# A vision tower with soft mixture-of-experts: logits made by slot from tokens scaled to unit length, dispatch and slot inputs one step later

## The chip, the cores and the metric

One core of a Trainium2 chip. The metric is the device time of one launch in microseconds (us), the median of several runs on the same chip. TensorE is called PE in the rows, VectorE DVE, ScalarE ACT, GpSimd POOL; SP issues transfers.

## What is computed

64 images of 3x224x224 are cut into 196 patches of 16x16 and embedded to 192 features; then come one attention with decay, one layernorm, and a soft mixture of 64 experts ("slots"), with one more layernorm. The change lies in the mixture:

```python
xn = _rms_norm(x, norm_weight, RMS_EPS)
tok = _l2_normalize(xn)
sl = _l2_normalize(slots) * scale[:, None]
logits = jnp.einsum('sd,btd->bst', sl, tok)
dispatch_w = jax.nn.softmax(logits, axis=-1)      # over the tokens
combine_w = jax.nn.softmax(logits, axis=-2)       # over the slots
y = jnp.einsum('btd,bst->bsd', xn, dispatch_w)
y = jnp.einsum('sio,bsi->bso', fc1_weight, y) + fc1_bias
y = jax.nn.gelu(y, approximate=False)
y = jnp.einsum('sio,bsi->bso', fc2_weight, y) + fc2_bias
out = jnp.einsum('bsd,bst->btd', y, combine_w)
```

In front of it: `h = layernorm(h + attention(h))`; behind it: `layernorm(h + out)`. All inputs and outputs are fp32.

## The kernel before

Three phases follow each other. **Phase 1** is a loop of 32 steps, each on one pair of images (392 tokens, in four tiles `t` of 98). It is written as a software pipeline: step `i` embeds pair `i` and runs its attention, projects out and normalizes pair `i-1`, and makes the logits and both softmaxes of pair `i-2`; some of the leftovers are of pair `i-3`. Steps 0 to 3 and 31 are written out, 4 to 30 are a hardware loop; a step's flags `c`, `d`, `e` say whether pairs `i-1`, `i-2`, `i-3` exist. **Drain** (`drain` on PE, the code behind `phase1` on the others) finishes the last two pairs, 30 (`one`) and 31 (`last`). **Phase 2** runs the 64 experts in 32 steps of two, each with 2.3 MB of weights from HBM through a ring of six buffers. **Phase 3** mixes the expert outputs back to the tokens and normalizes.

There is no scheduler: the order on each engine is the order of the code, an engine takes its instructions in that order, and engines meet by semaphores (`pe.wait_ge(hb_sb, i + 1)` holds PE and all that stands behind it). Matmul results lie in the eight banks of `ps`; a bank can be written again only when its reader is done, so many waits are for a copy on ACT or DVE.

The steps of the mixture for one pair, with the lines of before:

- `tokens` (DVE): `gn` = (t2 - mean) times the norm weight; `squares` (ACT, L679) sums its squares; `token_norms` and `cosine_scales` on DVE with powers on POOL (`token_scales`, `inverse_norms` L496) make `amp` (rms scale) and `cosc` (scale to unit length).
- `token_features` (PE, L1279): eight transposes of `gn` into banks 6 and 7; ACT copies them to `tokT`.
- `logits` (PE, L1288): per tile two products with 98 tokens stationary and 64 slots moving, so the result lies by token; `cosines` (DVE) multiplies by `cosc` into `Lt`; `logits_turned` (L1295) turns it by slot.
- `slot_maxima`, `slot_exponentials`: `Es` = exp(logits - max) by slot; `dispatch_turned` (L1301) turns `Es` to tokens, ACT copies it to `DT`; `slot_inputs` (L1309) is the product of `DT` with `xn` (the tokens times `amp`, made by `scaled_tokens` on POOL); ACT scales it to `ysb`; `slot_inputs_turned` (L1263, L1265) turns it for phase 2, and ACT copies it to `yT`.
- `shifted_logits`, `token_exponentials`, `token_sums`, `combine_weights`: the softmax over slots, `Cn`; `combine_turned` (L1272) turns it, ACT copies it to `cst` (L716), SP stores it.

Of the attention around them: `hb` (DVE, L1003) frees banks 6 and 7; `scores` (PE, L1210) three times a step, each followed by a `decay` (DVE, L927) of 98x1568 elements, each followed by `values` (PE, L1243); `gate` (PE, L1156) with its Tanh on ACT (`gt`, L656); `keys_turned` (L1217); `carried` (L1257). ACT also rounds x for the next pair in two halves (`round_x`, L595) and loads a function table twice a step (`use_table`, L607). `idle_products` are matmuls without a use, put into gaps of the drain.

Of the kernel before, what the change touches and what calls it, by code (L numbers as in the profile page):

```python
# [24 lines left out]
TOK = GRID * GRID  # L25
# [44 lines left out]
def vit_tower(nc, xT, W, Wq, Wk, Wv, Wo, Wg1, Wg2, log_slope, row_slope, ln_w, ln_b, slots, scale, fc1, fc1b, fc2, fc2b,  # L70
# [6 lines left out]
    with ExitStack() as ctx:  # L77
# [109 lines left out]
        ss, nra, nrb, nrm, invn, cosc = (sb(n, [T, 4]) for n in ("ss", "nra", "nrb", "nrm", "invn", "cosc"))  # L187
        expo = sb("expo", [128, 4, 4])
# [4 lines left out]
        Lt, Lc, Ec, Cn = (sb(n, [T, 4, S]) for n in ("Lt", "Lc", "Ec", "Cn"))  # L193
# [38 lines left out]
        nra_rdy, nrm_rdy, invn_rdy, cosc_rdy = (sem(n) for n in ("nra_rdy", "nrm_rdy", "invn_rdy", "cosc_rdy"))  # L232
        h2_stored = sem("h2_stored")
        tokT_mm, tokT_sb = sem("tokT_mm"), sem("tokT_sb")
        lg_mm, Lt_rdy, lneg_rdy = sem("lg_mm"), sem("Lt_rdy"), sem("lneg_rdy")
# [39 lines left out]
        def phase3(eng, step):  # L275

            for n in range(DEEP):
                step(n, n, 0)
            with eng.Fori(1, NP // DEEP) as w:
                for n in range(DEEP):  # L280
                    step(DEEP * w + n, n, w)

# [129 lines left out]
        def _(pool):  # L412
# [43 lines left out]
            def step(i, c, d, e, f, more):  # L456
# [5 lines left out]
                if d:  # L462
                    scaled_tokens(i - 2)
# [3 lines left out]
                if d:  # L467
                    inverse_norms(i - 2)
# [47 lines left out]
            def scaled_tokens(j):  # L516

                pool.wait_ge(ra_rdy, j + 1)
                pool.wait_ge(gn_rdy, 4 * j + 4)
# [63 lines left out]
        def _(act):  # L583
# [25 lines left out]
            def step(i, c, d, e, f, more):  # L609
# [9 lines left out]
                if d:  # L619
                    act.wait_ge(tokT_mm, i - 1)  # L620
                    act.activation(tokT[:, :, :], ps[0:G, 6:8, 0:PT], ACT.Copy).then_inc(tokT_sb, 1)
# [4 lines left out]
                act.activation(hTh[:, 1], hT[:, 1], ACT.Copy).then_inc(hTh_rdy, 1)  # L626
                if more:
# [916 lines left out]
```

## Time and profile before

| | |
|---|---|
| time, median of 3 runs | 1163.93 us (1162.79 to 1168.42) |
| the profiled execution | 1163.77 us, its span 1162.0 us |
| loop, 100 to 800 us: busy | PE 691.93, DVE 586.77, ACT 531.02, POOL 467.58 of 700; granted clock 1.00 |
| drain, 850 to 879 us: busy | PE 23.84, DVE 17.30, ACT 14.66, POOL 12.84 of 29; granted clock 0.98 |
| of it, 862 to 864 us | PE 0.70 of 2; granted clock 1.00 |
| experts, 879 to 1058 us: busy | PE 176.79 of 179; DMA share 0.95, 383 GB/s |
| last stage, 1058 to 1162 us: busy | DVE 80.39, ACT 59.54, POOL 56.92, PE 51.25 of 104 |

A row of a timeline gives start and duration in us, the engine, the line, the operation, what it writes and reads, and in brackets how long the engine had stood idle before it and for whom. An fp32 product with a 64x192 result counts as two matmuls there. Matmuls overlap, so the time that a group takes on PE is better read from its start to the start of the next group than from its duration.

### The profile page before, as it was taken

What the parts mean: (1) busy time and instruction counts of PE and PEld (TensorE: products, weight loads), DVE (VectorE), ACT (ScalarE), POOL (GpSimd) and SP (SyncE); (2) the same over time, 40 slices, a digit from 0 to 9 for tenths busy, and PEclk for the clock granted to TensorE, in tenths of its full rate; (3) what the DMA queues carried; (4) which work ended last, traced back from release to release, by engine and by line L of the source; (5) the groups of instructions that cost most, each with busy time, mean ns of one, the idle gap of its engine ahead of it and who ended that gap; (6) DMA issues with size and microseconds to landing.
All of it is one profiled execution on the core that took longest, in us unless ns stands there. A gap on an engine that the chain in (4) does not pass through costs nothing.

```text
span 1162.0 us, 35600 instructions
## 1 busy us (share of the span) xinstructions
PE 1080.2 (93%) x13250; PEld 853.4 (73%) x13250; DVE 839.9 (72%) x2118; ACT 725.5 (62%) x1712; POOL 633.6 (55%) x971
## 2 busy tenths in 40 slices
PE   7899999999999999999999999999998999996652
PEld 6688888888888888888888888888874555654331
DVE  5878888888888888888888888888872222223996
ACT  6457777777777777777777777777752111111666
POOL 4556666667666666667666666667641000001664
PEclk9999999999999999999999999999998999998555
DMA  4511221111111221111111221111085999995885
GB/s 160 206 54 54 87 70 66 55 55 55 55 55 55 81 75 66 55 55 55 55 55 55 79 77 66 55 55 55 15 344 183 421 424 424 423 415 151 254 256 178
DMA packets 50996, 158.50 MB, mean 136 GB/s; under 512 B 5659, under 2 KB 31665, under 8 KB 38645
## 3 DMA queue, kind: packets, MB, share of 16 engines
q1 hardware_dynamic: 33352, 145.11, 34.1%
q10 hardware_dynamic: 17600, 12.78, 3.5%
q8 instruction: 31, 0.51, 0.2%
q14 instruction: 13, 0.10, 0.0%
HBM read 132.25 MB, written 25.62 MB: 136 GB/s over the span
## 4 chain that ended last, share of the span: by engine, by line
PE 83%; DVE 8%; issue 3%; ACT 2%; POOL 1%; DVEq 1%; DMA 1%; ACTq 0%; SPq 0%; POOLq 0%
PE ps L1118 9%; PE ps L1119 8%; PE ps L1120 8%; PE ps L1210 7%; PE ps L1243 7%; PE ps L1439 6%; PE ps L1288 4%; PE ps L1458 4%; PE ps L1140 3%; PE ps L1194 3%; PE ps L1195 3%; DVE res L1088 2%; PE ps L1177 2%; PE ps L1463 2%; PE ps L1472 2%
## 5 line engine op out<-in xcount | busy, mean ns | idle before, releaser
L927 DVE TENSOR_TENSOR p_sb<-ps,dec 98x1568 f32<-98x1568 f32 x96 | 172.0, 1791 | 25.9 <-PE ps L1210 23.2
L436 POOL TENSOR_TENSOR xl<-x_sb,xh 128x392 fp32r<-128x392 f32 x186 | 188.2, 1040 | 0.0
L492 POOL TENSOR_TENSOR hTl<-hT,hTh 128x392 fp32r<-128x392 f32 x64 | 66.3, 1036 | 135.5 <-ACT hTh L693 103.0
L755 ACT ACTIVATE hg<-ps 128x768 f32<-128x768 f32 x32 | 25.9, 810 | 148.4 <-PE ps L1463 148.4
L875 DVE SCALAR_TENSOR_TENSOR t<-t,rstd,hb 98x192 f32<-98x192 f32 x128 | 85.9, 710 | 24.4 <-POOL rstd L503 24.4
L1080 DVE COPY y2st<-ps 128x192 f32<-128x192 f32 x32 | 11.4, 358 | 120.4 <-PE ps L1439 120.4
L552 POOL CAST pickb<-pick 128x128 fp32r (+1 forms) x32 | 9.4, 293 | 150.3 <-PE ps L1463 150.3
L530 POOL TENSOR_TENSOR Cn<-Ec,crec 98x256 f32<-98x256 f32 x32 | 20.7, 648 | 125.3 <-DVE crec L964 125.3
L1243 PE MATMUL ps<-p_sb,vpad 98*32 98x98 f32 x3072 | 85.6, 252 | 2.0 <-DVE p_sb L927 2.0
L772 ACT ACTIVATE o_sb<-res,nb,rstd 98x192 f32<-98x192 f32 x128 | 59.5, 535 | 44.4 <-DVE nb L1103 43.7
L1487 PE MATMUL ps<-y2b,cbuf 64*98 64x192 f32 x256 | 49.2, 536 | 37.6 <-POOL y2b L565 37.6
L1243 PEld LDWEIGHTS ps<-p_sb,vpad 98*32 98x32 f32 x3072 | 64.6, 110 | 26.4 <-issue 13.8
L607 ACT ACT_TABLE_LOAD x60 | 77.0, 1283 | 1.1
L595 ACT ACTIVATE xh<-x_sb 128x1176 fp32r<-128x1176 f32 x64 | 74.9, 1172 | 1.2 <-DMA x_sb<-in_xT 1.1
L686 ACT ACTIVATE h<-t,mur,ra 98x192 f32<-98x192 f32 x128 | 59.7, 538 | 23.5 <-DVE mur L907 21.8
L1487 PEld LDWEIGHTS ps<-y2b,cbuf 64*98 64x98 f32 x256 | 32.5, 266 | 54.1 <-issue 31.0
L1118 PE MATMUL ps<-xl,wh 128*128 128x392 f32 x192 | 69.6, 362 | 2.0 <-POOL xl L440 2.0
L1439 PEld LDWEIGHTS ps<-w2v,hgT 128*64 128x64 f32 x768 | 52.3, 137 | 25.9 <-issue 18.5
L1439 PE MATMUL ps<-w2v,hgT 128*64 128x192 f32 x768 | 69.5, 330 | 1.1 <-DVE hgT L1074 1.1
L1210 PE MATMUL ps<-qA,kA 32*98 32x196 f32 x1024 | 59.6, 345 | 10.1 <-ACT vpad L674 7.5
L1194 PE MATMUL ps<-xl,whl 128*128 128x392 f32 x192 | 68.1, 355 | 0.0
L523 POOL TENSOR_TENSOR xn<-gn,ra 98x192 f32<-98x192 f32 x128 | 68.1, 560 | 0.0
(221 smaller groups left out, 3443.6 us busy)
## 6 DMA issues: line engine op xcount, KB each, us to landing
x_sb<-in_xT SPq DMA_DIRECT2D x32, 1176.0 KB, 5.3
w1v<-in_fc SPq DMA_DIRECT2D x32, 1152.0 KB, 10.7
w2v<-in_fc SPq DMA_DIRECT2D x32, 1152.0 KB, 13.2
h_dram<-h SPq DMA_DIRECT2D x32, 294.0 KB
h2r<-h_dram SPq DMA_DIRECT2D x32, 294.0 KB
out<-o_sb ACTq DMA_DIRECT2D x32, 294.0 KB
comb_dram<-cst SPq DMA_DIRECT2D x32, 98.0 KB, 5.2
cbuf<-comb_dram SPq DMA_DIRECT2D x32, 98.0 KB, 4.0
```

The source lines that it names most:

```text
L436: pool.tensor_tensor(xl[:, k], x_sb[:, k], xh[:, k].bitcast(F32), ALU.subtract)\
L607: act.activation(warm[:, 1:2], warm[:, 0:1], func)
L875: dve.scalar_tensor_tensor(t2[0:T, t], t2[0:T, t], rstd1[:, t:t + 1], hb[0:T, t], ALU.mult, ALU.add).then_inc(t2_rdy, 1)
L927: dve.tensor_tensor(dst, src, rate.unsqueeze(2).to_broadcast([T, 4, 2, TOK]), ALU.mult)\
L1118: pe.matmul(out, hi, x_lo, start=start, stop=False)
L1119: pe.matmul(out, lo, x_hi, start=False, stop=False)
L1120: return pe.matmul(out, hi, x_hi, start=False, stop=stop)
L1194: pe.matmul(ps[:, 1, 0:PT], whl[:, k], xl[:, k], start=(k == 0), stop=False)
L1210: mm = pe.matmul(ps[0:T, SC_AT + r, mt * TOK:(mt + 1) * TOK].rearrange("p (b n) -> p b n", b=2), keys[rows, n], queries[rows, :, n], start ...
L1243: mm = pe.matmul(ps[32 * r:32 * r + 32, 6 + k // 2, at:at + T], vpad[:, 2 * a + mt, 32 * h:32 * h + 32], p_sb[:, k % 2, mt, (2 * r + odd) ...
L1439: mm = pe.matmul(ps[64 * s:64 * s + 64, 4 + n % 2, 0:D], hgT[:, k, at:at + 64], w2v[n][:, s, k], start=(k == 0), stop=(k == FJ - 1))
L1487: mm = pe.matmul(ps[0:T, 2 * n + a, k * D:(k + 1) * D], cbuf[64 * a:64 * a + 64, n, k * T:(k + 1) * T], y2b[64 * a:64 * a + 64, n, :], sta ...
```

## The change

- `cosines` and `Lt` are gone. POOL scales `gn` by `cosc` instead of `amp` (`unit_tokens` for `scaled_tokens`), so `xn` holds tokens of unit length; PE turns these, and the logits come out final. They are made by slot: 64 slots stationary, 196 tokens moving, two products for each of the two images (`logits(j, a)`), into bank 0.
- ACT copies the logits from bank 0 to `Es` (`logits_kept`); `slot_maxima` and the exponential work on `Es`; `logits_turned` now turns them to tokens into bank 1, for `shifted_logits`.
- The dispatch weights need the token's length back: DVE makes `size` in `cosine_scales`, and `dispatch_scaled` multiplies it into `DT` (it was a copy on ACT).
- In the loop `dispatch_turned` and `slot_inputs` of pair `i-3` move behind the two `project_out` calls of step `i`; `token_features` moves behind `hb`; `slot_inputs_turned` follows `combine_turned` between the turned keys and `scores` 1, and `gate` waits for ACT's copies of both; the turned keys go to bank 0; the second half of `round_x` moves behind Tanh on ACT.
- The drain is written anew: pair 29 ends there, pair 31 is scaled by DVE into `hb`, and the last `combine_turned` moves into the first expert step.

The core of the diff:

```diff
@@ POOL: step, unit_tokens @@
-                    scaled_tokens(i - 2)
+                    inverse_norms(i - 2)
                 low_h(i, 1)
                 if c:
                     first_norm(i - 1, 1)
                 if d:
-                    inverse_norms(i - 2)
+                    unit_tokens(i - 2)
...
-                    pool.tensor_tensor(xn[0:T, t], gn[0:T, t], amp[:, t:t + 1].to_broadcast([T, D]), ALU.mult)\
+                    pool.tensor_tensor(xn[0:T, t], gn[0:T, t], cosc[:, t:t + 1].to_broadcast([T, D]), ALU.mult)\
...
@@ POOL: drain @@
-            scaled_tokens(one)
+            unit_tokens(one)
             token_scales(last)
+            inverse_norms(last)
             combine_weights(one)
-            inverse_norms(last)
-            scaled_tokens(last)
             combine_weights(last)
@@ ACT: step @@
                 act.activation(hTh[:, 1], hT[:, 1], ACT.Copy).then_inc(hTh_rdy, 1)
+                if e:
+                    slot_inputs_scaled(i - 3)
...
+                if d:
+                    token_rows(i - 2)
                 if e:
-                    combine_kept(i - 3, 0, f)
-                if more:
-                    round_x(i + 1, 1)
+                    slot_inputs_kept(i - 3, 1, 0)
+                    combine_kept(i - 3, 1, f)
...
+                if more:
+                    round_x(i + 1, 1)
                 if d:
                     use_table(ACT.Exp)
+                    logits_kept(i - 2)
                     slot_exponentials(i - 2)
-                    if e:
-                        slot_inputs_kept(i - 3, 1, 0)
-                    dispatch(i - 2)
                     token_exponentials(i - 2)
...
+            def logits_kept(j):
+                act.wait_ge(lg_mm, j + 1)
+                if not (isinstance(j, int) and j == 0):
+                    act.wait_ge(dt_mm, j)
+                act.activation(Es[:, :], ps[:, 0, 0:TOK], ACT.Copy).then_inc(lg_sb, 1)
...
@@ ACT: drain, from the exponentials of pair 30 on @@
             token_exponentials(one)
             squares(last)
+            slot_inputs_scaled(one)
+            slot_inputs_kept(one, 5, 0)
             token_rows(last)
+            combine_kept(one, 4, True)
+            logits_kept(last)
+            slot_exponentials(last)
+            token_exponentials(last)
+            slot_inputs_scaled(last)
+            slot_inputs_kept(last, 5, 0)
             second_norm(last)
...
+            combine_kept(last, 6, True)
@@ DVE @@
+            def dispatch_scaled(j, norms):
+                dve.wait_ge(dt_mm, j + 1)
+                dve.wait_ge(size_rdy, j + 1)
...
+                dve.tensor_tensor(DT[:, :, :].rearrange("p k (a s) -> p k a s", a=2),
+                                  ps[0:T, 6, 0:256].rearrange("p (k a s) -> p k a s", k=2, a=2),
+                                  norms[:, :].rearrange("p (a k) -> p k a", a=2).unsqueeze(3)
+                                  .to_broadcast([T, 2, 2, S]), ALU.mult).then_inc(DT_sb, 1)
...
             for t in range(4):
+                dve.tensor_scalar(hb[0:T, t], gn[0:T, t], cosc[:, t:t + 1], None, ALU.mult).then_inc(xn_rdy, 1)
@@ PE: logits @@
-                        mm = pe.matmul(ps[0:T, 6 + t // 2, at:at + S], tokT[0:G, k, t * T:(t + 1) * T], slT[:, k, :],
-                                       start=(k == 0), stop=(k == 1))
+                for k in range(2):
+                    mm = pe.matmul(ps[64 * a:64 * a + 64, 0, 0:TOK], slT[:, k, :], tokT[0:G, k, a * TOK:(a + 1) * TOK],
+                                   start=(k == 0), stop=(k == 1))
@@ PE: step, from keys_turned on @@
                 if e:
-                    combine_turned(i - 3, 0)
+                    pe.wait_ge(zl_rdy, i + 1)
+                    pe.wait_ge(q_sb, 2 * i + 2)
+                    combine_turned(i - 3, 1)
+                    slot_inputs_turned(i - 3, 1, 0)
                 scores(i, 1, c)
+                pe.wait_ge(kts_rdy, i + 1)
                 if e:
+                    pe.wait_ge(yT_sb, 2 * i - 4)
                     pe.wait_ge(cb_sb, i - 2)
                 gate(i)
...
-                    logits_turned(i - 2)
+                    logits(i - 2, 0)
                 scores(i, 2, c)
+                if d:
+                    logits(i - 2, 1)
                 carried_ready(i)
                 values(i, 1)
...
                 carried(i, 0)
                 if d:
...
+                    logits_turned(i - 2)
                 values(i, 2)
...
                 carried(i, 1)
```

Where it moves instructions, as they stand in the loop. First PE behind `project_out` 0 (the products of woh and wol with og) and ahead of `embed` 1 (xl, xh with whl); before:

```order
L1177 MATMUL ps<-woh,ogl 98x192 x2
L1177 MATMUL ps<-woh,ogh 98x192 x2
L1276 ISA
L1279 MATMUL ps<-ident,gn 96x98 x8
L1194 MATMUL ps<-xl,whl 128x392
L1195 MATMUL ps<-xh,whl 128x392
```

After:

```order
L1194 MATMUL ps<-woh,ogl 98x192 x2
L1194 MATMUL ps<-woh,ogh 98x192 x2
L1317 MATMUL ps<-ident,Es 98x128 x2
L1211 MATMUL ps<-xl,whl 128x392
L1212 MATMUL ps<-xh,whl 128x392
```

Eight transposes of tokens are replaced by two of Es.

Second PE from `scores` 0 on (qA with kA); before:

```order
L1210 MATMUL ps<-qA,kA 98x196 x8
L1288 MATMUL ps<-slT,tokT 98x64 x8
L1217 MATMUL ps<-ident,kA 98x128 x2
L1218 MATMUL ps<-ident,kB 98x128
L1272 MATMUL ps<-ident,Cn 128x98 x2
L1204 ISA
L1210 MATMUL ps<-qA,kA 98x196 x8
L1156 MATMUL ps<-zs,gw 128x392
L1157 MATMUL ps<-zs,gw 64x392
L1243 MATMUL ps<-p_sb,vpad 32x98 x16
L1226 MATMUL ps<-vpad,kts 32x32 x12
L1295 MATMUL ps<-ident,Lt 128x98 x2
```

After:

```order
L1296 MATMUL ps<-ident,xn 96x98 x8
L1234 MATMUL ps<-ident,kA 98x128 x2
L1235 MATMUL ps<-ident,kB 98x128
L1289 MATMUL ps<-ident,Cn 128x98 x2
L1280 MATMUL ps<-ident,ysb 128x128
L1282 MATMUL ps<-ident,ysb 64x64 x2
L1221 ISA
L1227 MATMUL ps<-qA,kA 98x196 x8
L1381 REGISTER_ALU
L1173 MATMUL ps<-zs,gw 128x392
L1174 MATMUL ps<-zs,gw 64x392
L1260 MATMUL ps<-p_sb,vpad 32x98 x16
```

Between `scores` 0 and 1 the turned tokens and the turned ysb stand where the eight products of the logits stood; the new logits follow further on, ahead of and behind `scores` 2.

Third ACT from the second half of q (qB) to the Exp table; before:

```order
L645 ACTIVATE qB<-ps,parity 64x196 x4
L714 ISA
L716 ACTIVATE cst<-ps 128x196
L595 ACTIVATE xh<-x_sb 128x1176
L656 ACTIVATE gt<-ps 128x392
L659 ACTIVATE gt<-ps 64x196 x2
L607 ACT_TABLE_LOAD
```

After:

```order
L646 ACTIVATE qB<-ps,parity 64x196 x4
L674 ACTIVATE tokT<-ps 96x784
L731 ISA
L731 ACTIVATE yT<-ps 128x2x64
L731 REGISTER_ALU
L731 ACTIVATE yT<-ps 128x2x32
L724 REGISTER_ALU
L726 ACTIVATE cst<-ps 128x196
L658 ACTIVATE gt<-ps 128x392
L661 ACTIVATE gt<-ps 64x196 x2
L597 ACTIVATE xh<-x_sb 128x1176
L609 ACT_TABLE_LOAD
```

tokT and yT come ahead of cst, and the rounding of x goes behind Tanh.

## Rows read from the trace of the kernel before

**Rows 1.** Timeline of PE, one step; columns as told under the profile.

```profile
526.60 1.60 PE L1288 MATMUL ps<-slT,tokT 96*98 96x64 f32 x16
528.04 0.38 PE L1217 MATMUL ps<-ident,kA 128*98 128x128 f32 x2
...
529.48 0.44 PE L1156 MATMUL ps<-zs,gw 80*128 80x392 f32 x1
...
531.04 0.39 PE L1295 MATMUL ps<-ident,Lt 98*128 98x98 f32 x2
531.46 0.92 PE L1210 MATMUL ps<-qB,kB 32*98 32x196 f32 x16
...
533.13 0.33 PE L1263 MATMUL ps<-ident,ysb 128*128 128x128 f32 x1
...
533.66 0.54 PE L1257 MATMUL ps<-qd,state 32*32 32x98 f32 x16
534.13 0.43 PE L1301 MATMUL ps<-ident,Es 128*98 128x128 f32 x2
534.49 0.88 PE L1243 MATMUL ps<-p_sb,vpad 98*32 98x98 f32 x32
535.30 0.87 PE L1309 MATMUL ps<-xn,DT 98*64 98x192 f32 x8
536.10 0.37 PE L1257 MATMUL ps<-qd,state 32*32 32x98 f32 x8
...
540.79 0.88 PE L1279 MATMUL ps<-ident,gn 98*96 98x98 f32 x8
541.45 0.42 PE L1194 MATMUL ps<-xl,whl 128*128 128x392 f32 x1
```

**Rows 2.** Timelines of DVE and PE in step 0, and one decay of the steady step.

```profile
27.59 1.79 DVE L927 TENSOR_TENSOR p_sb<-ps,dec 98x1568 f32<-98x1568 f32 x1 [0.19 <-PE ps L1210]
...
35.27 0.89 PE L1243 MATMUL ps<-p_sb,vpad 98*32 98x98 f32 x32 [0.79 <-DVE p_sb L927]
...
526.63 1.79 DVE L927 TENSOR_TENSOR p_sb<-ps,dec 98x1568 f32<-98x1568 f32 x1
```

**Rows 3.** Timeline of ACT in the same step as rows 1.

```profile
526.08 1.47 ACT L645 ACTIVATE qB<-ps,parity 64x196 f32<-64x196 f32 x4
528.80 0.33 ACT L716 ACTIVATE cst<-ps 128x196 f32<-128x196 f32 x1 [1.25 <-PE ps L1272]
529.03 1.18 ACT L595 ACTIVATE xh<-x_sb 128x1176 fp32r<-128x1176 f32 x1
530.10 0.49 ACT L656 ACTIVATE gt<-ps 128x392 f32<-128x392 f32 x1
...
531.15 1.28 ACT L607 ACT_TABLE_LOAD   x1
...
533.85 0.51 ACT L721 ACTIVATE yT<-ps 128x128 f32 x2 [0.81 <-PE ps L1265]
...
542.61 0.81 ACT L621 ACTIVATE tokT<-ps 96x784 f32<-96x784 f32 x1
```

**Rows 4.** Timeline of DVE in step 0, a tensor-scalar operation.

```profile
35.04 0.35 DVE L825 TENSOR_SCALAR woh<-wo 128x384 fp32r<-128x384 f32 x1
```

**Rows 5.** Timelines of PE and DVE in the drain and the first expert step.

```profile
863.30 0.43 PE L1301 MATMUL ps<-ident,Es 128*98 128x128 f32 x2 [1.38 <-ACT Es L697]
...
868.55 0.16 DVE L899 TENSOR_TENSOR nra<-ss,ra 98x4 f32<-98x4 f32 x1 [3.70 <-ACT ysq L679]
...
871.41 0.46 DVE L911 TENSOR_TENSOR cosc<-ra,invn 98x4 f32<-98x4 f32 x1 [1.69 <-POOL invn L496]
...
878.19 0.56 PE L1272 MATMUL ps<-ident,Cn 98*128 98x98 f32 x2 [1.10 <-POOL Cn L530]
...
880.17 2.83 PE L1458 MATMUL ps<-w1v,yT 128*64 128x384 f32 x8
```

**Rows 6.** Windows: stretch, its length, busy PE, PEld, DVE, ACT, POOL, granted clock, DMA.

```profile
878.00:879.00 1.00, 0.56 (x2) 0.29 (x2) 0.00 (x0) 0.16 (x1) 0.88 (x5) 0.53 0.00 0
```

More of the change, by code:

```diff
@@ L1045, in _ @@
                 dve.tensor_tensor(ogl[:, n], og[:, n], ogh[:, n].bitcast(F32), ALU.subtract).then_inc(ogl_rdy, 1)
+            dispatch_scaled(one - 1, size)
             tokens(one)
@@ L1050, in _ @@
             residual(last, 0)
-            cosine_scales(one)
-            cosines(one)
+            cosine_scales(one, size)
             residual(last, 1)
@@ L1055, in _ @@
             residual_statistics(last, 1)
+            tokens(last)
             slot_maxima(one)
-            tokens(last)
+            shifted_logits(one)
             slot_sums(one)
-            shifted_logits(one)
             token_norms(last)
+            dispatch_scaled(one, size)
             mean_shifts(last)
             token_sums(one)
-            cosine_scales(last)
-            cosines(last)
+            cosine_scales(last, size_last)
+            dve.wait_ge(cosc_rdy, NP)
+            for t in range(4):
+                dve.tensor_scalar(hb[0:T, t], gn[0:T, t], cosc[:, t:t + 1], None, ALU.mult).then_inc(xn_rdy, 1)
             slot_maxima(last)
@@ L1067, in _ @@
             slot_sums(last)
+            dispatch_scaled(last, size_last)
             token_sums(last)
@@ L1183, in embed @@
                     pe.wait_ge(g_sb, 2 * i - 1 + g)
-                if e and g == 1:
-                    pe.wait_ge(y_sb, i - 2)
+                if e:
+                    pe.wait_ge((lg_sb, Lc_rdy)[g], i - 2)
                 for k in range(KP):
@@ L1333, in step @@
                     project_out(i - 1, 0)
-                if d:
-                    token_features(i - 2)
+                if e:
+                    dispatch_turned(i - 3)
                 embed(i, 1, c, e)
@@ L1338, in step @@
                     project_out(i - 1, 1)
+                if e:
+                    slot_inputs(i - 3, xn)
                 if at_start(i):
@@ L1389, in drain @@
                 one, last = NP - 2, NP - 1
-                idle_products(0, 8)
+                pe.wait_ge(og_sb, 2 * NP)
+                dispatch_turned(one - 1)
+                idle_products(0, 7)
                 project_out(last, 0)
-                token_features(one)
+                slot_inputs(one - 1, xn)
                 project_out(last, 1)
-                combine_turned(one - 1, 0)
-                slot_inputs_turned(one - 1, 0, TOK)
-                logits(one)
-                idle_products(1, 6)
+                pe.wait_ge(Lc_rdy, one)
+                combine_turned(one - 1, 1)
+                slot_inputs_turned(one - 1, 1, 0)
+                idle_products(0, 6)
+                token_features(one, xn)
+                idle_products(0, 4)
+                logits(one, 0)
+                logits(one, 1)
+                pe.wait_ge(t1_rdy, 4 * NP)
+                idle_products(2, 2)
+                pe.wait_ge(yT_sb, 2 * one)
                 pe.wait_ge(cb_sb, one)
-                pe.wait_ge(yT_sb, 2 * one)
                 logits_turned(one)
-                idle_products(1, 8)
+                idle_products(2, 5)
                 dispatch_turned(one)
-                idle_products(1, 2)
-                slot_inputs(one)
-                pe.wait_ge(t1_rdy, 4 * NP)
+                idle_products(2, 2)
+                slot_inputs(one, xn)
+                idle_products(2, 2)
                 slot_inputs_turned(one, 5, 0)
-                idle_products(2, 8)
-                token_features(last)
+                idle_products(2, 3)
+                token_features(last, hb)
                 idle_products(2, 4)
-                logits(last)
+                logits(last, 0)
+                logits(last, 1)
                 combine_turned(one, 4)
-                idle_products(2, 2)
+                pe.wait_ge(Lc_rdy, one + 1)
                 logits_turned(last)
```

161 lines of the change are left out of this document (69 added, 92 removed).

## The prediction, made before the changed kernel ran

> **What bounds the kernel now.** I read the page first: its slices and the share of TensorE say that the first 850 us, a loop of 32 steps of some 26 us, keep TensorE busy without a break. Then I read one step in the timeline of TensorE [rows 1] and looked, for every break between its stretches, at what the other engines had just finished. The reader is to see two kinds of stretch in it. From `values` 2 at 534.49 through both `embed` calls to the projections, matmuls follow each other with no gap: whatever is taken out there shortens the step by as much. From the end of `hb` (where `logits` starts, 526.60) to `values` 2 (534.49) lie 7.89 us in which DVE runs three `decay` operations of 1.79 us, each waiting for `scores` and each waited for by the next `scores` or `values`. Step 0, where TensorE has little else to do, shows what that chain takes alone: from 27.59, where the first decay starts, to 35.27, where `values` 2 starts, 7.68 us [rows 2]; in the steady step the same stretch takes 7.86, from the decay at 526.63 [rows 2] on. So this window is 0.18 above its floor: filled with work on TensorE, and nearly as long without it. I call it the window; zero of its clock is 526.60.
>
> **What the change does to the path outside the window.** `token_features` leaves it: 540.79 to 541.45, 0.66. `dispatch_turned` comes in behind `project_out` 0: 534.13 to 534.49, 0.36. `slot_inputs` goes from behind `values` 2 to behind `project_out` 1: 535.30 to 536.10, 0.80, on the path in either place. Together -0.30 us a step. Nothing covers these products, so the gain is real if TensorE finds no new wait there. The new waits: `slot_inputs` needs DT, which is now a DVE multiplication of 256 columns behind `first_norm` 0 (the multiplication that made Lt, of the same size, goes); between `dispatch_turned` and `slot_inputs` TensorE runs `embed` 1 and `project_out` 1, over 3 us (from 541.45 on), and the multiplication has room. `h_turned` 1 needs `y_sb`, behind `hTh` on ACT, with the first half of the projections as cover. On POOL the scaling of four tiles moves behind `low_h` 1 and the inverse norms in front of it; POOL is busy two thirds of the time there, and the scaled tokens are wanted only after `hb`. I cost all these at nothing; without cover the DT wait would cost about what it now hides, up to 0.5 a step.
>
> **What it does inside the window.** Out go the old `logits` (526.60 to 528.04: 1.44) and the turning of Lt (531.04 to 531.46: 0.42). In come `token_features` (0.66) and the new `logits`: four products of a 64-column stationary tile with 196 moving columns instead of eight with 64. The nearest row is `slot_inputs`, four products of 64 stationary and 192 moving columns: 0.80. One pair of transposes of Es (0.36) leaves and another takes its place. TensorE's work in the window falls by 0.40, to 7.49. But 7.49 is under the 7.68 of the decays, so no more than 0.18 can be had here, and two new round trips to ACT decide how much:
>
> First, `gate` now waits until ACT has copied tokT, yT and cst. qB ends at 526.08 + 1.47 = 0.95 on the window's clock; tokT 0.81 more: 1.76 [rows 3]. TensorE ends `slot_inputs_turned` at 0.66 + about 0.55 (turned keys and combine weights: 528.04 to 529.48 less the 0.9 of `scores`) + 0.53 (533.13 to 533.66) = 1.75; yT began 0.19 after that point before, so 1.94, plus 0.51 and 0.33: 2.7 to 2.8, and with a hand-off 2.85. Before, `gate` started at 529.48 = 2.88. Even.
>
> Second, `logits_turned` needs the copy of the logits, behind two Tanh, the rounding of x and the table load on ACT. From `gate`: 0.62 to Tanh (530.10), 1.05 to the end of both (531.15), 1.07 for x (529.03 to 530.10), 1.28 and a little more for the table, 0.33 for a copy like cst: 7.3, with a hand-off 7.45. TensorE gets there at 2.85 + 1.56 (529.48 to 531.04) + 0.40 + 1.67 (531.46 to 533.13) + 0.40 + 0.47 (533.66 to 534.13) = 7.35. It waits 0.1, turns the logits in 0.36 and starts `values` 2 at 7.83 against 7.89.
>
> So the window gives -0.06, between -0.18 (the decays alone) and whatever ACT is late by. A step is 0.36 shorter. The 29 steps from 3 to 31 have it in full, step 2 has only the 0.66 of `token_features`: 29 x 0.36 + 0.66 = **11.1 us** off the loop; with -0.18 in the window 29 x 0.48 + 0.66 = 14.6.
>
> Here the Trainium skill speaks against a simple reading: "Trainium Kernel Development and Optimization", section Performance Expectations, calls the busy time of matmuls a bad metric, because they are pipelined. By busy time alone the 0.7 a step taken from TensorE would all be gain, 20 us; by the rule a busy TensorE proves no bound at all, and the change could be worth nothing (the second rival is that case). The decays of [rows 2] side with the rule inside the window and not outside it.
>
> **The last passage** (from the loop's end to the first weights). For the last pair the order is now serial: norms, scaling, turning, copy, logits, copy, where before turning and logits ran beside the norms. From cosc on there are four scalings on DVE, 0.66 of transposes, tokT 0.81, logits 0.80 and a copy 0.33. A scaling of 192 columns lies under the 0.35 of 384 columns [rows 4], over the 0.16 of a 4-column row [rows 5]; I take 0.27, 1.1 for four. With five hand-offs and the idle products in between that is 5.4, less 0.5 for the multiplication it replaces: +4.9. Against it, cosc comes sooner: DVE waited 3.70 for the squares and 1.69 for the inverse norms [rows 5], both of which now stand ahead of work for pair 30 on ACT and POOL; I estimate -2.8 of these 5.4. The turning of the last combine weights (a wait of 1.10, and about 0.5 more for cst) moves into the first weights' products: -1.6; added idle products ahead of the end: +1.7. The granted clock had fallen to 0.53 by 878 to 879 [rows 6], and the eight first weights' products at 880.17 took 2.83 [rows 5]. With idle products in the gaps I expect the full level and half the time for them and their like: -2.2. Then ACT, ahead of the first Gelu: four h2 rows, cst, the table load (1.28, [rows 3]): +1.3. Sum +1.3; nearer to +1 since the loop's last `slot_inputs` no longer stands ahead of the last og.
>
> One gap in it is new: pair 30's scaled tokens come from POOL only after its cosc, and I make TensorE idle there for nearly 3 us, against 1.38 at 863.30 [rows 5], after which the granted clock stayed at 1.00 (the table of the profile section), and 1.10 at 878.19, by when it had fallen. I take it that the clock falls there to the lower level, 1.2 instead of 2.4 GHz: turning and logits at twice their 0.66 and 0.80 and idle products in front of them, some +2. So the passage costs **+3 us**, with bounds of -2 (no fall, nearly all 5.4 of the waits gone) and +6.
>
> The Trainium skill, "VectorE: DVE Perf Modes", section Mode 2x_2P, lets an fp32 tensor-scalar run at two results a cycle; the 0.35 for 384 columns agrees. By it the four scalings would be some 0.3 us cheaper.
>
> After that nothing changes: the weights' products and the last stage start later or earlier as a block, since each transfer of weights follows a product. The comb store moves behind the first products; its reload was issued some 10 us ahead of use.
>
> **Sum.** Profiled execution 1163.77 (span 1162.0; the median of the three runs is 1163.93, the same): 1163.8 - 11.1 + 3 = **1155.7 us**.
>
> **Rivals.**
> 1. The window reaches its floor and the clock does not fall: 1163.8 - 14.6 + 0 = 1149. For it: the work is under the floor. Against: the margin at the two round trips is 0.1.
> 2. The window grows by what the outside gives. ACT now does three copies between qB and Tanh and the rounding of x between Tanh and the table; hand-offs of 0.1 more at each, or DVE late for `hb`, put `values` 2 at 8.1 to 8.2 instead of 7.83. Then a step gains 0 to 0.1 and the passage is left: 1163.8 - 2 + 1 = 1163, within 0.5%.
> 3. Slower: ACT takes over the window. Each 0.1 by which `gate` comes after 2.85 moves `scores` 2, the last decay and `values` 2 by 0.1. From a `gate` at 3.2 on the loop gains nothing; at 3.5, if tokT, yT and cst each need a further 0.2, a step is 0.3 longer: 1163.8 + 29 x 0.3 - 0.66 + 1 = 1173. The rows have tokT behind qB without a gap, so I hold it unlikely.
> 4. The logits are not cheaper: at their old 1.44 TensorE would need 8.13 in the window, +0.24 against 7.89, and the step would gain 0.06: 1165, even. The row of `slot_inputs` speaks against it.
>
> **How the numbers follow.** Forecast 0.50, first rival 0.16, second and fourth 0.24, third 0.10. The range takes in the bounds of window and passage and the second rival, and leaves out the third and the edge of the first: 1147 to 1165. A difference of 0.5%, 5.8 us, is about what a measurement here can tell from none. Faster than 1158: most of the forecast and the first rival, 0.65; within: 0.25; slower than 1169.7: 0.10.
>
> **What would show it.** In the step after: the time from one step's `logits` to the next's 0.36 less; `token_features` behind `hb` without a wait; `gate` 2.85 after it; ACT's copy of the logits just ahead of `logits_turned`; no wait ahead of `slot_inputs`. In the passage: a TensorE gap near 3 us ahead of pair 30's `token_features` with the granted clock falling behind it, and the first weights at full clock. Wrong: waits of TensorE for ACT of more than 0.2 in each step, or the first weights' products not some 7 us earlier than 880.17.

## The result, and the profile after

The changed kernel takes 1191.26 us (median, 1190.01 to 1192.63) where the kernel before took 1165.84 (1162.79 to 1168.42) beside it: a ratio of 1.0216, interval 1.0194 to 1.0238. It is slower by some 25 us; the forecast was 1155.7, in a range of 1147 to 1165. The profiled execution of after has a span of 1188.3 us.

One steady step on PE, timeline of after (as [rows 1]), from the end of `hb`:

```profile
514.97 0.88 PE L1296 MATMUL ps<-ident,xn 98*96 98x98 f32 x8 [0.90 <-DVE hb L1018]
...
517.63 0.41 PE L1173 MATMUL ps<-zs,gw 80*128 80x392 f32 x1
...
519.15 0.88 PE L1303 MATMUL ps<-tokT,slT 96*64 96x196 f32 x4
519.96 0.92 PE L1227 MATMUL ps<-qB,kB 32*98 32x196 f32 x16
520.81 0.88 PE L1303 MATMUL ps<-tokT,slT 96*64 96x196 f32 x4
521.62 0.89 PE L1260 MATMUL ps<-p_sb,vpad 98*32 98x98 f32 x32
...
522.91 0.42 PE L1311 MATMUL ps<-ident,Es 128*98 128x128 f32 x2
523.26 0.89 PE L1260 MATMUL ps<-p_sb,vpad 98*32 98x98 f32 x32
...
528.79 0.42 PE L1317 MATMUL ps<-ident,Es 128*98 128x128 f32 x2
528.97 0.42 PE L1211 MATMUL ps<-xl,whl 128*128 128x392 f32 x1
...
540.10 0.92 PE L1227 MATMUL ps<-qA,kA 32*98 32x196 f32 x16 [0.23 <-ACT vpad L686]
...
541.92 0.87 PE L1296 MATMUL ps<-ident,xn 98*96 98x98 f32 x8 [0.91 <-DVE hb L1018]
```

The rows of before that go with it, besides [rows 1], are `values` 2 of one step and `scores` 0 of the next:

```profile
508.32 0.88 PE L1243 MATMUL ps<-p_sb,vpad 98*32 98x98 f32 x32
...
525.66 0.92 PE L1210 MATMUL ps<-qA,kA 32*98 32x196 f32 x16 [0.23 <-ACT vpad L674]
```

A step takes 541.92 - 514.97 = 26.95 us; before it took 26.2 (from `values` 2 at 508.32 to 534.49). Three stretches make the difference of about +0.77:

- The window, from the end of `hb` (514.97) to `values` 2 (523.26): 8.29, against 7.89 in [rows 1]: **+0.40**. The two halves of `logits` take 0.81 each, 519.15 to 519.96 and 520.81 to 521.62, together 1.62.
- From `values` 2 to the next `scores` 0 (540.10): 16.84, against 17.34 before (508.32 to 525.66): **-0.50**.
- From `scores` 0 to the end of the wait for `hb` (541.92): 1.82, against 0.94 before: **+0.88**, a wait of 0.9 that was not there. The waits of PE from 300 to 800 us list it in 18 steps (us in total, times, longest):

```profile
PE ps L1296 <- DVE hb L1018: 16.3, 18, 0.9
```

Why DVE is late with `hb` stands in the same step's timelines of DVE and of POOL:

```profile
504.63 0.75 DVE L883 SCALAR_TENSOR_TENSOR t<-t,rstd,hb 98x192 f32<-98x192 f32 x2
...
507.33 0.81 DVE L920 TENSOR_TENSOR cosc<-ra,invn 98x4 f32<-98x4 f32 x1
...
510.23 2.17 DVE L883 SCALAR_TENSOR_TENSOR t<-t,rstd,hb 98x192 f32<-98x192 f32 x2 [0.38 <-POOL rstd L507]
512.33 0.61 DVE L889 BATCH_NORM_STATS2 st<-t 98x6 f32<-98x192 f32 x2
...
513.88 0.96 DVE L1018 TENSOR_TENSOR hb<-ps,lnb 98x768 f32<-98x768 f32 x1
```

```profile
504.61 1.01 POOL L500 TENSOR_TENSOR invn<-nrm,expo 98x4 f32<-98x4 f32 x1
507.08 1.04 POOL L496 TENSOR_TENSOR hTl<-hT,hTh 128x392 fp32r<-128x392 f32 x1 [1.46 <-ACT hTh L625]
509.15 0.19 POOL L505 TENSOR_TENSOR ve<-mv,expo 98x2 f32<-98x2 f32 x1 [1.03 <-DVE mv L871]
...
510.08 2.07 POOL L526 TENSOR_TENSOR xn<-gn,cosc 98x192 f32<-98x192 f32 x4
512.11 3.12 POOL L440 TENSOR_TENSOR xl<-x_sb,xh 128x392 fp32r<-128x392 f32 x3
```

`cosc` has four columns and took 0.153 in every steady step before; here it starts at 507.33, inside POOL's `hTl`, and ends with it, 0.81 later. What follows it on DVE comes later, POOL waits 1.03 for `mv`, and residual 1 waits for POOL's `rstd`. Then residual 1 itself, two tiles, takes 2.17 beside POOL's scaling; before, residual 1 took 1.51 and residual 0, which had the scaling beside it then, 1.15. The statistics at 512.33, with one operand in SBUF, take 0.61 beside POOL's `xl`, as they did without it.

Running side by side does not settle it alone. In the same step residual 0 takes only 0.75 for its two tiles (504.63) while POOL's inverse norms run (504.61, 1.01). And in every steady step of before `cosc` too starts inside an operation of POOL, the first of the three of `xl`, but 0.13 ahead of its end, and comes through. DVE in one step of before, then that one operation of POOL:

```profile
522.51 1.51 DVE L875 SCALAR_TENSOR_TENSOR t<-t,rstd,hb 98x192 f32<-98x192 f32 x2
...
524.80 0.15 DVE L911 TENSOR_TENSOR cosc<-ra,invn 98x4 f32<-98x4 f32 x1
```

```profile
523.77 1.16 POOL L436 TENSOR_TENSOR xl<-x_sb,xh 128x392 fp32r<-128x392 f32 x1
```

In the last passage the gap of nearly 3 us is there, and the first weights' products are at full clock (1.51, against 2.83 in [rows 5]). The granted clock stayed at 1.00 (4 us from 884) behind that gap and fell behind the next. Timeline of PE, then windows with the columns of [rows 6]:

```profile
885.08 0.88 PE L1296 MATMUL ps<-ident,xn 98*96 98x98 f32 x8 [2.98 <-POOL xn L526]
886.87 0.89 PE L1303 MATMUL ps<-tokT,slT 96*64 96x196 f32 x8
892.46 0.87 PE L1324 MATMUL ps<-xn,DT 98*64 98x192 f32 x8 [1.99 <-DVE DT L928]
...
907.00 1.51 PE L1482 MATMUL ps<-w1v,yT 128*64 128x384 f32 x8
```

```profile
884.00:888.00 4.00, 2.92 (x26) 2.43 (x27) 2.70 (x12) 1.00 (x2) 3.08 (x6) 1.00 1.00 424
892.00:896.00 4.00, 3.54 (x23) 2.82 (x24) 2.59 (x11) 0.92 (x3) 1.59 (x2) 0.71 0.40 150
```

From `values` 2 of the last step to the first turning of `hg` the passage takes 38.5 us (872.91 to 911.44), before 36.9 (848.49 to 885.41): +1.6. The loop has lost 24.4 (`values` 2 of the last step at 872.91 instead of 848.49); 24.4 + 1.6 = 26.0, and the spans differ by 26.3.

One more row matters here. In the passage both halves of `logits` stand together, and all four products take 0.82 from their start to the next group's (886.87 to 887.69): as much as one half alone in the loop.

### The profile page after: what moved, and what is told of

Read it like the earlier page. It is cut to its first block, busy times and chain, and to the rows that moved or that the text cites. A ratio compares the mean times of both kernels' runs of the same rounds, so it can differ in the third digit from the quotient of the medians.

```text
span 1188.3 us, 35236 instructions
## 1 busy us (share of the span) xinstructions
PE 1076.5 (91%) x13008; PEld 837.5 (70%) x13008; DVE 862.8 (73%) x2154; ACT 738.8 (62%) x1711; POOL 628.2 (53%) x967
## 4 chain that ended last, share of the span: by engine, by line
POOL 36%; issue 27%; PE 22%; DVE 10%; ACT 2%; DVEq 1%; DMA 1%; POOLq 1%; ACTq 0%; SPq 0%
POOL xl L440 14%; PE ps L1463 6%; POOL xn L526 5%; PE ps L1482 4%; POOL ra L517 4%; POOL hTl L496 4%; POOL rstd L507 2%; DVE res L1103 2%; POOL invn L500 2%; PE ps L1498 2%; DVE st L1109 2%; PE ps L1489 2%; POOL qd L477 1%; DVE p_sb L947 1%; PE ps L1227 1%
## 5 line engine op out<-in xcount | busy, mean ns | idle before, releaser
L883 DVE SCALAR_TENSOR_TENSOR t<-t,rstd,hb 98x192 f32<-98x192 f32 x128 | 93.1, 767 | 15.9 <-POOL rstd L507 15.5
L1463 PEld LDWEIGHTS ps<-w2v,hgT 128*64 128x64 f32 x768 | 52.3, 137 | 25.8 <-issue 18.5
L1133 PE MATMUL ps<-wvl,hTh 128*98 128x192 f32 x256 | 67.3, 263 | 0.2 <-DVE t L876 0.2
## 6 DMA issues: line engine op xcount, KB each, us to landing
w1v<-in_fc SPq DMA_DIRECT2D x32, 1152.0 KB, 11.1
```

The lines of the kernel that those rows point to most:

```text
L883: dve.scalar_tensor_tensor(t2[0:T, t], t2[0:T, t], rstd1[:, t:t + 1], hb[0:T, t], ALU.mult, ALU.add).then_inc(t2_rdy, 1)
L1133: pe.matmul(out, hi, x_lo, start=start, stop=False)
L1463: mm = pe.matmul(ps[64 * s:64 * s + 64, 4 + n % 2, 0:D], hgT[:, k, at:at + 64], w2v[n][:, s, k], start=(k == 0), stop=(k == FJ - 1))
```

## The experiments

My theory of the two losses: the halves of `logits` write different 64-column halves of the array and run side by side only when they are adjacent; and a DVE operation with two SBUF operands does not get through while POOL works on SBUF (the rows of residual 0 and of before's `cosc` show that this is too broad as it stands). The rivals: a product costs what it costs wherever it stands; and DVE is late because it has more operations in its queue.

**e1_join**: the two halves together.

```diff
+                scores(i, 2, c)
                 if d:
                     pe.wait_ge(g_sb, 2 * i + 1)
                     logits(i - 2, 0)
-                scores(i, 2, c)
-                if d:
                     logits(i - 2, 1)
```

> Both halves of the logits stand together behind the scores of the third heads, instead of one ahead of them and one behind. Theory A (two products that write different 64-column halves of the array run side by side when they are adjacent, and only then): the four products take 0.8 together as in the last passage, TensorE's work in the window falls by 0.8, the third scores start 0.45 earlier, and the window from the token features to values 2 falls from 8.29 to about 7.85; 29 steps x 0.45 = -13, about 1178 us. Theory B (a product costs 0.2 to 0.4 wherever it stands, and the window is long because of ACT's round trips): the four take 1.6 in their new place, and the time stays within 3 us of 1191.

Measured: 1179.39 us, ratio 1.0121 (1.0078 to 1.0164). Timeline of PE in the window:

```profile
432.47 0.92 PE L1227 MATMUL ps<-qB,kB 32*98 32x196 f32 x16 [0.26 <-DVE p_sb L947]
433.32 0.89 PE L1303 MATMUL ps<-tokT,slT 96*64 96x196 f32 x8
434.14 0.89 PE L1260 MATMUL ps<-p_sb,vpad 98*32 98x98 f32 x32
...
435.79 0.89 PE L1260 MATMUL ps<-p_sb,vpad 98*32 98x98 f32 x32
```

The four products take 0.82 together, though the code has both products of one half ahead of both of the other, and with `token_features` at 427.96 the window is 7.83 (to 435.79): theory A, 12 us of the 25.

**e2_cosc_early**: `cosine_scales` ahead of the statistics of residual 0, so ahead of POOL's `hTl`; on DVE nothing is added or removed.

```diff
+                if d:
+                    cosine_scales(i - 2, size)
                 if c:
                     residual_statistics(i - 1, 0)
-                if d:
-                    cosine_scales(i - 2, size)
```

> The inverse norms times amplitudes (cosc, size) are computed on DVE right behind the sum of h, ahead of the statistics of residual 0, so before POOL begins its low half of h; nothing is added or taken away on DVE. Theory A (cosc takes 0.80 because it runs against POOL's low half of h, and all of DVE up to hb is late by that): cosc takes 0.15, TensorE's wait of 0.90 for hb goes from 0.90 to 0.3 or less, a step gets 0.6 to 0.9 shorter, 29 x 0.6 to 0.9 = -17 to -26 us, 1165 to 1174. Theory B (DVE is late because two more small operations and the wait for POOL's inverse norms stand in its queue, wherever they stand): cosc still takes 0.8 or DVE waits for the inverse norms as long, and the time stays within 4 us of 1191.

Measured: 1173.6 us, ratio 1.0064 (1.0043 to 1.0086). `cosc` between 300 and 800 us (duration in ns: least, median, most), and PE's wait for `hb`:

```profile
L920 DVE TENSOR_TENSOR cosc<-ra,invn x19: 161/164/165, 311.1 to 784.1; 98x4 f32<-98x4 f32 x19
```

```profile
529.19 0.87 PE L1296 MATMUL ps<-ident,xn 98*96 98x98 f32 x8 [0.25 <-DVE hb L1018]
```

The same operation, 0.8 us earlier in the queue: 0.164 instead of 0.80, and a step 0.66 shorter (`scores` 0 from 501.74 to 528.02: 26.28). So it was its place beside POOL and not its being there.

**e3_join_cosc**: both edits.

> Both edits of the two runs before it. If the two losses are separate, one ahead of the window and one in it, the gains add: 29 x (0.45 + 0.6 to 0.87) = -30 to -38 us, 1153 to 1161, below the kernel before, near the forecast of 1155.7. If one of them only hides the other, the sum falls short of that by the smaller one: 1166 to 1178.

Measured: 1158.01 us (1157.31 to 1159.74), ratio 0.9932 (0.991 to 0.9954): faster than before, and 2.3 us from the forecast. PE:

```profile
495.55 0.87 PE L1296 MATMUL ps<-ident,xn 98*96 98x98 f32 x8 [0.25 <-DVE hb L1018]
...
503.38 0.89 PE L1260 MATMUL ps<-p_sb,vpad 98*32 98x98 f32 x32
...
521.37 0.88 PE L1296 MATMUL ps<-ident,xn 98*96 98x98 f32 x8 [0.24 <-DVE hb L1018]
```

The window is 7.83 and the step 25.82. From `values` 2 of step 0 to `values` 2 of step 31 the loop takes 804.2 us (34.78 to 839.00), after 836.7, e1 823.2, e2 816.8: -13.5 and -19.9 singly, -32.5 together. The two losses are separate.

**e4_same_half**: e1 with both halves on the same 64 columns of the array. The copy to `Es` still reads the old places, so half of the logits in its output are not those asked for.

```diff
-                    mm = pe.matmul(ps[64 * a:64 * a + 64, 0, 0:TOK], slT[:, k, :], tokT[0:G, k, a * TOK:(a + 1) * TOK],
+                    mm = pe.matmul(ps[0:64, 0, 256 * a:256 * a + TOK], slT[:, k, :], tokT[0:G, k, a * TOK:(a + 1) * TOK],
```

> As the run with both halves of the logits together, but both halves write the same 64 columns of the array (at other places of the bank); the copy reads the old places, so half of the logits in the output are not those asked for. Theory A (adjacent products on different column halves overlap): the four products take 1.6 from start to start again, though adjacent, and the time is about 1190. Theory C (what overlaps is only the latency of products that stand next to each other): they take 0.8 as with different halves, and the time is that of the run with both halves together.

Measured: 1200.18 us (one run). PE:

```profile
414.79 1.54 PE L1303 MATMUL ps<-tokT,slT 96*64 96x196 f32 x8
416.26 0.89 PE L1260 MATMUL ps<-p_sb,vpad 98*32 98x98 f32 x32
```

Adjacent, but on the same columns, they take 1.47. So it needs both: different column halves, next to each other. The time is 9 us above after, not at it as I expected. Some 6 of them lie in the loop (842.8 from `values` 2 of step 0 to that of step 31, in after 836.7): behind `scores` 2 the pair leaves PE waiting 0.27 for DVE's decay ahead of them, and in after the first half stood there. Another 4 lie in the last passage (42.65 against 38.5), which has the same edit and in which the granted clock fell twice.

**e10_join_ahead**: e3 with the pair ahead of `scores` 2.

> As e3_join_cosc, but both halves of the logits stand ahead of the scores of the third heads instead of behind them. Theory A (what the join saves is TensorE's work, 0.8 a step, wherever the pair stands): scores 2 start 0.55 later, but values 1 follow them at once, values 2 start within 0.1 of where they did, and the time is within 3 us of 1158. Theory B (what the join saves is that scores 2, and so the last decay on DVE, start earlier): the window grows by 0.4 to 0.55 a step again, 1170 to 1174.

Measured: 1161.18 us (1158.55 to 1164.63), ratio 0.9967 (0.9954 to 0.998). In its trace `scores` 2 start 0.48 later in the window than in e3, and `values` 2 at the same 7.83 (499.72 to 507.55). What the join saves is PE's work, not the place of `scores` 2; 1170 is ruled out. A step takes 0.06 more than e3's, and its wait for `hb` is 0.30 instead of 0.24. Of the 5.7 us between the two profiled executions 3.5 lie ahead of `values` 2 of step 0 (38.24, in e3 34.78), ahead of anything that the edit moves; whether the 3 us between the medians come from there is not shown.

**e7_pool_yields**: e3, and POOL waits in each step until residual 1 is done.

```diff
                 if c:
                     first_norm(i - 1, 1)
+                    pool.wait_ge(t2_rdy, 4 * i)
                 if d:
                     unit_tokens(i - 2)
```

> On top of e3_join_cosc: in each step POOL waits until DVE has done residual 1 before it scales the tokens; no work changes. Theory A (DVE's residual of two SBUF operands gets through only when POOL stands still, 1.1 for one beside the scaling against 0.41 alone): residual 1 takes 0.75 to 0.85 instead of 2.17, POOL starts the scaling 0.8 later, and TensorE's wait of 0.24 for hb goes to 0 to 0.1; 29 x 0.15 to 0.24 = -4 to -7 us, 1151 to 1154. Theory B (the residual is slow for another reason, such as its operands from ACT or PSUM traffic): it keeps its 2.17, hb waits as before, the scaling comes 2 later and the token features wait for POOL: above 1165.

Measured: 1152.47 us (1151.27 to 1157.12), ratio 0.9897 (0.9866 to 0.9927). The time is as expected and the place of the gain is not. Residual 1 takes 0.75 in every step and the wait for `hb` is gone from the list, but the steady step still takes 25.8: the first decay starts 0.98 after `scores` 0 in both kernels (516.75 after 515.77, 521.19 after 520.21), so it had waited for `scores`, and 0.24 of waiting for `hb` beside it cost nothing. From step 0 to 31 the gain is 5.5 us, and 4.5 of them lie in step 1, where POOL runs `xl` right behind `rstd`. DVE and POOL in step 1 of after, then DVE in step 1 of e7:

```profile
50.11 3.15 DVE L883 SCALAR_TENSOR_TENSOR t<-t,rstd,hb 98x192 f32<-98x192 f32 x1 [0.30 <-POOL rstd L507]
```

```profile
50.04 3.00 POOL L440 TENSOR_TENSOR xl<-x_sb,xh 128x392 fp32r<-128x392 f32 x3
```

```profile
49.50 0.75 DVE L884 SCALAR_TENSOR_TENSOR t<-t,rstd,hb 98x192 f32<-98x192 f32 x2 [0.31 <-POOL rstd L508]
```

One tile took 3.15 us beside three POOL operations in a row, and two take 0.75 without them.

**e9_before_yields**: the same wait in the kernel before, ahead of its first `split_x`.

> The kernel before with one wait more: in each step POOL waits until DVE has done residual 1 before it forms the first remainders of x. In the trace of e7_pool_yields the gain came in step 1 alone (residual 1 of step 1 took 3.83 beside those remainders and 0.75 with the wait), not in each step, and the trace of before has the same 3.83. Theory A (that loss belongs to both kernels, and the change under study has no part in it): the kernel before gains 3 to 4.5 us, to about 1162, so of e7's lead over before only what e3 has is the change's. Theory B (the wait only helps together with the scaling on POOL): within 1 us of before.

Measured: 1425.87 us (1369 to 1437, so that even the quickest of four is 204 above before): a large loss that neither theory named. Step 1 gains as expected (its residual 1 takes 0.75), and the other steps lose far more. DVE, POOL and PE in one step of the execution that took 1418.3 us:

```profile
632.76 3.30 DVE L913 TENSOR_TENSOR cosc<-ra,invn 98x4 f32<-98x4 f32 x1
```

```profile
632.50 2.98 POOL L436 TENSOR_TENSOR xl<-x_sb,xh 128x392 fp32r<-128x392 f32 x3
635.44 0.60 POOL L475 TENSOR_TENSOR qd<-qA 128x196 f32<-128x196 f32 x1
```

```profile
637.70 2.61 PE L1290 MATMUL ps<-slT,tokT 96*98 96x64 f32 x16 [2.27 <-DVE hb L1005]
```

The wait lets `xl` start behind residual 1 instead of beside it, so that `cosc`, two operations further on DVE, comes 0.26 behind the start of `xl`'s first operation and not, as in before, 0.13 ahead of its end. It takes 3.30, until the fourth POOL operation in a row ends; PE stands for 2.27; and behind such gaps the granted clock falls to the lower level. The gap of the step ahead took 2.35 and ended at 601.98; behind it the clock was low for some 17 us, 604 to 621. Windows from that gap on:

```profile
604.00:606.00 2.00, 2.00 (x18) 1.42 (x18) 1.12 (x3) 1.41 (x2) 0.43 (x2) 0.50 0.00 0
...
620.00:622.00 2.00, 2.00 (x10) 2.00 (x9) 1.38 (x5) 1.29 (x3) 0.00 (x0) 0.75 0.00 0
622.00:624.00 2.00, 2.00 (x22) 1.78 (x21) 0.40 (x2) 1.36 (x5) 0.26 (x1) 1.00 0.49 151
```

**e11_before_step1** and **e12_join_cosc_step1**: the wait in step 1 alone (`if c and not d:`), in the kernel before and in e3.

> The kernel before with POOL's wait for residual 1 in step 1 alone. Theory A (the 3.83 of residual 1 in step 1 is a loss of both kernels, and the 260 us of e9 came from the other steps, where the wait pushes POOL's remainders of x onto DVE's small cosc, 3.29 there): residual 1 of step 1 takes 0.75, step 1 ends 3 to 4 earlier, the rest is as before: 1161 to 1163. Theory B (the kernel before has cover for it): within 1 us of before.

> e3_join_cosc with POOL's wait for residual 1 in step 1 alone. Theory A (the wait of 0.24 for hb in the steady step hides nothing, since the first decay waits for the scores, and e7's gain was step 1's and step 2's): 3 to 4 us less than e3, 1153.5 to 1155, and the steady step as in e3. Theory B (e7 also gained in each step): no more than 1 us under e3's 1158.

Measured: e11 1161.9 us, ratio 0.9976 (0.9964 to 0.9989); e12 1154.41, ratio 0.9919 (0.9897 to 0.9941). Both as theory A had it: from `values` 2 of step 0 to that of step 31, e11 is 3.1 us under before (810.1 against 813.2), and e12 4.6 under e3 (799.6). The loss in step 1 belongs to both kernels; what the change and its two repairs bring by themselves is e3's 0.68%.

**e5_dve_scale** and **e6_squares_first**: the last passage, on top of e3. In e5 DVE scales pair 30 right behind `cosc`, with the `tensor_scalar` that pair 31 has. In e6 ACT makes the squares of pair 31 ahead of its copy of pair 30's logits.

```diff
@@ POOL @@
-            unit_tokens(one)
@@ DVE @@
             cosine_scales(one, size)
+            dve.wait_ge(cosc_rdy, NP - 1)
+            dve.wait_ge(y_mm, one)
+            for t in range(4):
+                dve.tensor_scalar(xn[0:T, t], gn[0:T, t], cosc[:, t:t + 1], None, ALU.mult).then_inc(xn_rdy, 1)
@@ ACT @@
             token_rows(one)
+            squares(last)
             logits_kept(one)
             slot_exponentials(one)
             token_exponentials(one)
-            squares(last)
```

> On top of the join and the early cosc (e3_join_cosc): in the last passage pair 30's four scalings go from POOL (2.19 in that run's trace, 851.12 at their end) to DVE right behind cosc (1.01 there for pair 31's), ahead of the last residual. Theory A (the passage is a chain, and TensorE's gap ahead of pair 30's token features is all POOL's scaling): the gap of 2.99 goes to 1.4 to 1.7, and if the granted clock then stays at 1.00, the 0.50 level of 852 to 856 goes too: from values 2 of the last step to the first turning of hg 39.74 becomes 36.3 to 38.3. Theory B (the chain of squares and norms of pair 31, pushed back 1 us on DVE, ends last): TensorE waits as much more at DT behind it, and the 39.74 stays within 0.5.

> On top of e3_join_cosc: in the last passage ACT makes the squares of pair 31 ahead of its copy of pair 30's logits instead of behind the exponentials. Theory A (TensorE's wait of 1.99 for DT is a wait for these squares, through the norms that stand ahead of DT on DVE): the wait goes to 0.3 to 0.6 and the passage of 39.74 to about 38.2. Theory B (the wait is the exponentials', turning and DVE multiplication's own latency): it stays above 1.5, and the copy of the logits behind the squares comes later.

Measured, one run each: 1155.78 and 1153.94 us. The passage, 39.7 in e3, takes 36.4 in e5 and 36.75 in e6. PE in e5, then in e6:

```profile
853.15 0.88 PE L1299 MATMUL ps<-ident,xn 98*96 98x98 f32 x8 [1.75 <-DVE xn L1066]
```

```profile
857.73 0.87 PE L1324 MATMUL ps<-xn,DT 98*64 98x192 f32 x8
```

The gap of 2.99 is 1.75 in e5, and the granted clock is 1.00 from 848 to 862. In e6 the wait for DT (1.99) is gone; the passage gains 3.0 where I had expected 1.5. Part of that goes with the clock, which came back sooner (0.50 for 852 to 854 only, in e3 from 852 to 856): e1 and e7, which have e3's passage, took 38.5 for it without either edit, and against these e5 gains 2.1 and e6 1.8. Of e5's shorter passage less is left in its time, since `values` 2 of step 0 comes at 38.32 there, 3.5 later than in e3, ahead of anything that the edit moves.

**e8_all**: e3 with the edits of e5, e6 and e7.

> The three edits before it together on top of e3_join_cosc. If they are separate: -4 to -7 in the loop, -1.4 to -3.4 and -1.6 in the last passage: 1146 to 1151 us. If POOL's later scaling only moves the wait (to its rounding remainders of x at the next embedding), the loop gives nothing and the time is 1153 to 1156.

Measured: 1148.63 us (1147.04 to 1150.17), ratio 0.9857 (0.9835 to 0.9878). The loop from step 0 to 31 is e7's (798.7 us), the passage 35.7, shorter than the 36.9 of before: e5 and e6 together take 4.1 off e3's, singly 3.3 and 3.0. It beats both kernels.

## Why the prediction was wrong, point by point

**The logits, inside the window: the size was wrong.** The step said "In come `token_features` (0.66) and the new `logits`", priced at 0.80 by the row of `slot_inputs`. That row (535.30 to 536.10 in [rows 1]) is of four products that alternate between the column halves without a break. The change puts `scores` 2 between its halves, and split they take 1.62, not twice the 0.40 that the prediction's sum for `logits_turned` has. With the products joined the window is 7.83 (e1, e3); with them split it is 8.29. That 7.83 is also the forecast, to the hundredth, is luck: in e3 PE comes to `token_features` 0.24 late, and so the count starts later against the decays. In e7, without that wait, the same stretch takes 7.95:

```profile
516.79 0.88 PE L1297 MATMUL ps<-ident,xn 98*96 98x98 f32 x8
...
524.74 0.89 PE L1261 MATMUL ps<-p_sb,vpad 98*32 98x98 f32 x32
```

Nor is PE held there by ACT's copy of the logits, as the prediction had it: it waits for the second decay ahead of `scores` 2 (0.26 in e1 and e3), and from there to `values` 2 its products follow each other without a break. The Trainium skill, "TensorEngine Tiling (Array Packing)", section Performance Considerations, offers twofold column tiling for a stationary side of up to 64; e1 and e3 agree (0.82 for four), and e4 and the split halves show when it does not come: on the same columns (1.47), or with other work between (1.62). The fourth rival had this case in kind (the logits at their old 1.44) and put it at +0.24 a step; it was +0.40.

**DVE and POOL: "I cost all these at nothing" failed.** It was the larger half, +0.88 a step, of which e2 gives back 0.66 by moving `cosc`. The reason given, that POOL is busy two thirds of the time, is about free time; what counts is which two operations meet, and when. The order of after puts the inverse norms ahead of `low_h` 1 on POOL, has `cosc` ahead of residual 1 on DVE, where its turn comes 0.25 behind the start of `hTl`, and puts the scaling beside residual 1. The Trainium skill, "SBUF — State Buffer", section Who interferes with whom, states that a DVE instruction with two SBUF inputs contends with a GpSimd instruction that reads SBUF; of DVE's two-port modes it adds that whoever issues first has the shared ports for the whole instruction and the other is blocked. e2, e7 and e9 agree that they contend (0.164 against 0.80 and 3.30 for one operation). The measurements differ from the page in two ways, and they decide: the page speaks of one instruction, and the 3.30 lasted through four; and residual 0, two SBUF inputs as well, was not held by the inverse norms (0.75 for two tiles at 504.63). Why these do not hold it is open. The rule speaks against this change and the prediction did not weigh it, and the trace of before shows such holding too: grouped over its whole trace, the 128 residual operations there read

```profile
L875 DVE SCALAR_TENSOR_TENSOR t<-t,rstd,hb x128: 410/655/3146, 43.8 to 860.1; 98x192 f32<-98x192 f32 x128
```

The same shape takes 0.41 to 3.15 us. A spread of 1 to 8 in one operation was the warning. The second rival does speak of "DVE late for `hb`", as one of several causes that together would make the window 0.3 longer and leave the step as it was.

**Outside the window: right in sign, too small.** -0.50 a step instead of -0.30. `dispatch_turned` takes 0.18 from its start to the next group's (528.79 to 528.97), not 0.36: in [rows 1] the 0.36 stands between `carried` and `values`.

**ACT's round trips: right.** `gate` starts 2.66 after `token_features` (2.85 was forecast) and `logits_turned` does not wait. The third rival, ACT taking the window, did not happen.

**The last passage: right, by a range.** +3 with bounds of -2 and +6; the profile of after has +1.6, e2 and e3 with the same code +2.8 to +2.9. The gap before pair 30's `token_features` is 2.98. The fall of the clock behind it came in e2 and e3 and not in after.

**The sum.** Forecast -11.1 for the loop and +3 for the passage. With the two losses repaired e3 has -9.0 (813.2 to 804.2 from `values` 2 of step 0 to that of step 31) and +2.8. That its step, 25.82, is the forecast's 26.17 - 0.36 is partly luck: outside the window it gains 0.51 instead of 0.30, and ahead of `token_features` it loses 0.22 that was not forecast (1.16 from `scores` 0 on, before 0.94). The miss of after is made of the terms above: a window of +0.40 for -0.06, the wait of 0.88 for nothing, and -0.50 for -0.30 outside give 29 x (0.46 + 0.88 - 0.20) = 33.1 by the step shown. All 29 steps, from `values` 2 of step 2 to that of step 31, take 780.4 against 758.8, 21.6 more where 10.4 less was forecast: 32.1. The steps 0 to 2 add 3.4 (`values` 2 of step 2 starts at 92.47 instead of 89.68, 2.8 later where 0.66 sooner was forecast), and the passage takes 1.4 less than forecast. 1155.7 + 32.1 + 3.4 - 1.4 = 1189.8, and the profiled execution of after took 1190.0.

## What to carry to other kernels

Price a moved product by a row in which it has the same neighbours: four products, two on each column half, took 0.82 together and 1.62 in two pieces. When work is moved on POOL, list for each DVE operation with two SBUF operands what POOL does at that time; the smallest operation can be held longest, and a spread of durations in one group of the trace is the sign. A wait on PE that the trace names (0.24 for `hb`) is worth nothing when another engine waits beside it for something else, as e7 showed.

## What the runs showed of the hardware, unexpected

A DVE operation of 98x4 with two SBUF operands was held 3.30 us, through four POOL operations in a row, not only through the one that ran when it started; one of 98x192 was held 3.15 beside three. Beside the four shorter scalings (0.51 each) a residual came through after two (1.08 and 1.17). The moment of the meeting counts with it: the 98x4 operation that was held 3.30 in e9, where it came 0.26 behind the start of `xl`, took 0.15 in before, where it came 0.13 ahead of the end of `xl`'s first operation.

The granted clock was not the same behind the gap of 2.98 us in the last passage, with the same matmuls around it: in e2 and e3 it was near 0.5 as soon as the gap ended (0.54 and 0.57 over the 2 us with its end), in e1 and e7 it fell 1 to 2 us later, and in after it held 1.00 to the next gap. The passage took 39.7 to 39.8 in the first two and 38.5 in the others. What decides there was not settled. The gap of 2.35 us in e9 was followed by some 17 us at 0.50, and the slices of its page have 7 or 8 tenths nearly all through the loop.
